# An earlier load of the third pair of heads, and a projection one step later in causal attention

## The reference

```python
x = LN(x + L0_attn(x))          # one wide attention with rotary embedding, K = 512
x = LN(x + L0_xattn(x, ctx, ctx, gamma))
#   q, k, v are [B, 512, 512]; 8 heads over the first axis (64 rows each):
#   qk = einsum('bhdq,bhdl->bhql', qh, kh) / sqrt(64); softmax; einsum('bhql,bhdl->bhdq', sm, vh)
x = LN(x + L0_ffn(x))           # ternary weights, 8-bit activations, Hadamard transform
x = LN(x + L1_attn(x))
#   kqv = x @ Wqkv + bqkv; 16 heads of 32
#   scores = einsum('bsnh,btnh->bnst', k, q) / sqrt(32)
#   scores = triu(scores) + -10000 * tril(ones, k=-1); softmax over axis 2; @ v; @ Wo + bo
x = LN(x + L1_xattn(x, ctx, mask))
x = LN(x + L1_ffn(x))           # 4-bit weights
```

## Time and profile before

| | |
|---|---|
| three runs, median | 1651.87 us (1650.08 to 1654.97) |
| the profiled execution, its own time | 1652.51 us |
| its span | 1650.7 us |
| mean granted TensorE clock | 0.981 |
| PE busy | 1546.3 us (94%) |
| DVE busy | 1276.7 us (77%) |
| ACT busy | 950.2 us (58%) |
| POOL busy | 761.9 us (46%) |

### The profile page before, as it was taken

The page is one execution under the profiler, slowest core; times in us unless marked ns, Lnnn a source line. Parts: engine busy times, 40 slices in busy tenths (PEclk is TensorE's granted clock), DMA queues, the critical chain, the costliest instruction groups (busy, mean ns, idle before and its releaser), DMA issues. The chain is left out here.

```text
span 1650.7 us, 25463 instructions
## 1 busy us (share of the span) xinstructions
PE 1546.3 (94%) x8236; PEld 1105.7 (67%) x8268; DVE 1276.7 (77%) x2288; ACT 950.2 (58%) x1980; POOL 761.9 (46%) x729
## 2 busy tenths in 40 slices
PE   8999998999987999999898999999899999999996
PEld 5788876666644566666666767676467767777774
DVE  6467665777989999997677687887779989767573
ACT  3212224787876677677566666666535555555654
POOL 5043255777832454452622233233144266656564
PEclk9999999999999999999997999999999999999998
DMA  7200016643220000003422122222243100000000
GB/s 229 77 1 26 1 51 172 211 129 117 65 77 1 1 1 1 2 1 77 117 77 59 57 77 58 59 77 65 66 119 96 47 1 1 1 26 26 1 26 26
DMA packets 66998, 95.95 MB, mean 58 GB/s; under 512 B 11956, under 2 KB 28852, under 8 KB 66868
## 3 DMA queue, kind: packets, MB, share of 16 engines
q1 hardware_dynamic: 60196, 81.47, 16.2%
q0 software_dynamic: 6144, 12.60, 2.9%
q10 hardware_dynamic: 528, 0.26, 0.1%
HBM read 56.53 MB, written 4.19 MB: 37 GB/s over the span
## 5 line engine op out<-in xcount | busy, mean ns | idle before, releaser
L1929 ACT ACTIVATE causal_probs<-bank,causal_neg 128x512 f32<-128x512 f32 (+3 forms) x256 | 134.4, 530 | 129.1 <-DVE causal_neg L2023 104.0
L3202 PE MATMUL bank<-fp_xT,fp_weights_values 128*128 128x512 f32 x704 | 187.7, 403 | 7.4 <-DVE fp_gate L3096 5.1
L3202 PEld LDWEIGHTS bank<-fp_xT,fp_weights_values 128*128 128x128 f32 x704 | 128.2, 188 | 55.0 <-DVE fp_gate L3096 12.3
L1196 POOL DMA_DIRECT2D causal_qS<-causal_qk x96 | 48.7, 514 | 190.3 <-DVE causal_qk L1188 143.0
L3229 PE MATMUL bank<-fp_wd,fp_hT 128*128 128x512 f32 x528 | 133.7, 393 | 1.4 <-POOL fp_hT L2919 1.1
L3105 DVE SCALAR_TENSOR_TENSOR fp_up<-bank,fp_weights_scales,fp_up 128x512 f32<-128x512 f32 x132 | 99.1, 751 | 44.8 <-ACT fp_up L2988 37.4
L892 DVE TENSOR_REDUCE heads_neg<-bank 128x1 f32<-128x512 f32 x128 | 86.3, 676 | 42.0 <-PE bank L943 41.8
L3229 PEld LDWEIGHTS bank<-fp_wd,fp_hT 128*128 128x128 f32 x528 | 98.5, 188 | 25.7 <-issue 3.4
L1627 PE MATMUL bank<-weights_raw,ternary_qT 128*128 128x512 bf16 x432 | 103.9, 386 | 6.2 <-DVE ternary_z L1468 5.4
L1255 POOL TENSOR_TENSOR ternary_z<-ternary_z 128x1024 f32<-128x1024 f32 x16 | 38.8, 2426 | 152.2 <-DVE ternary_z L1468 143.0
L355 POOL TENSOR_TENSOR rope_qk<-rope_rot 128x512 f32<-128x512 f32 x32 | 43.0, 1342 | 142.8 <-DVE rope_rot L458 141.3
(11 more groups left out here) (289 smaller groups left out, 4270.2 us busy)
## 6 DMA issues: line engine op xcount, KB each, us to landing
pairs_xd<-X SPq DMA_DIRECT2D x64, 128.0 KB, 2.6
pairs_cd<-in_ctx SPq DMA_DIRECT2D x64, 128.0 KB, 2.7
causal_qS<-causal_qk SPq DMA_DIRECT2D x96, 64.0 KB, 2.7
causal_qS<-causal_qk POOLq DMA_DIRECT2D x96, 64.0 KB, 2.5
causal_kS<-causal_qk SPq DMA_DIRECT2D x96, 64.0 KB, 2.7
causal_kS<-causal_qk POOLq DMA_DIRECT2D x96, 64.0 KB, 2.6
X<-in_x SPq DMA_DIRECT2D x4, 1024.0 KB, 6.8
heads_cT<-in_ctxT SPq DMA_DIRECT2D x4, 1024.0 KB, 5.7
```

Of the source, the lines that this page charges most:

```text
L1929: act.activation(probs_of(i)[:, h + one], view[:, one], ACT.Exp, bias=neg[:, G % 2, at:at + 1], accum_out=total[:, G % 2, at:at + 1]).then ...
L3202: last = pe.matmul(banks[4 + g][:], values[:, g, n % NI, of], xT[:, part, g], start=part == 0, stop=part == 1)
```

## The change

Two things. The third pair's load moves from the second stage's SP stream to the end of the first stage's; it waits for `stacked >= 1`, since it goes into pair 0's slot. And for G = 4, 8, 12 the queries' thirds are done in steps 1, 2, 3 in place of 0, 1, 2; ACT's high and DVE's low part of q follow in step 4 in place of 3. The keys stay in 3, 4, 4. `late` goes; the order of the streams is otherwise unchanged. Within ACT's step the high part stands behind the copies of turned tiles and ahead of the exponentials; within DVE's step the low part stands behind the maxima.

```diff
@@ rope_attention, SP
             pairs.load(sp, 0)
             pairs.load(sp, 1)
+            sp.wait_ge(pairs.stacked, 1)
+            pairs.load(sp, 2)
@@ head_attention, SP
             for g in range(PAIRS):
                 b, pair = divmod(g, NT)
-                if g >= 2:
+                if g >= 3:
                     sp.wait_ge(pairs.stacked, g - 1)
                     ...
                     pairs.load(sp, g)
@@ causal_attention
     PROJECT = ((0, 1, 2), (3, 4, 4))
+    PROJECT_NEXT = ((1, 2, 3), (3, 4, 4))
...
-        def late(G):
-            return 0
+        def thirds(G, j):
+            return (PROJECT if G % NF else PROJECT_NEXT)[j]
@@ ACT
-                if G + 1 < GROUPS and k - late(G + 1) in (PROJECT[0][-1] + 1, PROJECT[1][-1] + 1):
-                    first.high(act, G + 1, ...)
+                for j in range(2):
+                    if G + 1 < GROUPS and k == thirds(G + 1, j)[-1] + 1:
+                        first.high(act, G + 1, j, bank_of(G + 1, j))
@@ DVE
-                if G + 1 < GROUPS and k - late(G + 1) in (PROJECT[0][-1] + 1, PROJECT[1][-1] + 1):
-                    first.low(dve, G + 1, ...)
+                for j in range(2):
+                    if G + 1 < GROUPS and k == thirds(G + 1, j)[-1] + 1:
+                        first.low(dve, G + 1, j, bank_of(G + 1, j))
@@ PE
                 if G + 1 < GROUPS:
                     for j in range(2):
                         for third in range(3):
-                            if k == PROJECT[j][third] + late(G + 1):
+                            if k == thirds(G + 1, j)[third]:
                                 project(G + 1, j, third)
```

More of the change, by code:

```diff
@@ L1960, in _ @@
                         keep((n - TURN[u] - 1) // STEPS, u)
-                if G + 1 < GROUPS and k - late(G + 1) in (PROJECT[0][-1] + 1, PROJECT[1][-1] + 1):
-                    first.high(act, G + 1, (PROJECT[0][-1] + 1, PROJECT[1][-1] + 1).index(k - late(G + 1)), bank_of(G + 1, (PROJECT[0][-1] + 1, PROJECT[1][-1] + 1).index(k - late(G + 1))))
+                for j in range(2):
+                    if G + 1 < GROUPS and k == thirds(G + 1, j)[-1] + 1:
+                        first.high(act, G + 1, j, bank_of(G + 1, j))
                 for f in range(NF):
@@ L2090, in _ @@
                         keep(G, 0)
-                if G + 1 < GROUPS and k - late(G + 1) in (PROJECT[0][-1] + 1, PROJECT[1][-1] + 1):
-                    first.low(dve, G + 1, (PROJECT[0][-1] + 1, PROJECT[1][-1] + 1).index(k - late(G + 1)), bank_of(G + 1, (PROJECT[0][-1] + 1, PROJECT[1][-1] + 1).index(k - late(G + 1))))
+                for j in range(2):
+                    if G + 1 < GROUPS and k == thirds(G + 1, j)[-1] + 1:
+                        first.low(dve, G + 1, j, bank_of(G + 1, j))
                 for past_b, t, half in out_at(n):
```

## The result

Six runs of the changed kernel have a median of 1641.65 us (1640.24 to 1642.82), six of the kernel before beside them 1650.97 (1645.79 to 1654.97). The ratio is 0.9947, 95% interval 0.9932 to 0.9961: by the ratio 8.7 us faster, between 6.4 and 11.2 (the medians lie 9.3 apart). A second measurement in another session gave 0.9953 (0.9937 to 0.9970). Of the 4.8 us between the forecast and the median, 0.9 lie in the median before: the forecast started from 1651.87, of three runs, and six gave 1650.97.

The account below looks back on a forecast made before the run. PE was taken to bound both stages touched. The earlier load (-4.4) and later queries (-1.1) summed to -5.5 us: 1647.0 from the profiled 1652.51, expected median 1646.4, range 1642.8 to 1649.8 (forecast's own 1645 to 1648).

Parts of the forecast that it names:

- part 1: Head attention: the earlier third-pair load removes PE's 3.16 us wait at pair 2 and its slowness; -4.4 us in sum.
- the slow pair 2: Head attention: pair 2 takes 13.86 us, 1.23 more than in rhythm; this goes with the low clock.
- Rival C: Head attention: pair 3 takes the wait over, its loads behind 3 MB; gives back up to 3, 1649.5 us; chance 0.08.
- the forecast's own rule: Clock: about 3.7 us at low level cost 1.23, so a 6.7 us stretch costs 2.2 to 3.35 us.
- the end of the wait did not move: Causal attention, G = 4: x_low comes as before, so PE can't begin the first third before 872.30; 6.08 gain excluded.
- For G = 8 and 12 0.3 each: Causal attention: moved score and transposes gain 0.6 us per group; q's later low part leaves about 0.3 each.
- the copies at G = 4: First score of G = 4 waits for SP's k copies, which can move forward by 0.2 us or so.
- the step "That leaves 0.5 for G = 4": Causal attention, G = 4: the step keeps some 1.0 us, but k copies at the group's end leave 0.5.
- B: Rival: both parts at full and clock returns at G = 4, worth 1.2 to 1.7; -8.1, 1643.8 us; chance 0.20.
- low clock in other stretches, more than 3 us in sum: Sign that the forecast is wrong: low clock elsewhere than before, with more than 3 us in sum.

Follow-up runs that it names:

- experiment 4: Changed kernel with the queries' thirds in steps 1, 2, 2 or in steps 2, 2, 3 in place of 1, 2, 3: ratios 0.9965 and 0.9968 to the kernel before.
- after_fill: Changed kernel plus two useless matmuls in PE's wait ahead of the first projection of G = 4: ratio 0.9968 to the kernel before.
- experiment 3: Useless matmuls in the hole at G = 4: five in the kernel before 0.9989, two in the changed kernel 0.9968, five with the early load 0.9948.
- load_only: Kernel before with only the earlier load of the third pair: ratio 0.9970 to the kernel before, about -5.0 us.
- load_fill: Kernel before with the earlier load and five useless matmuls ahead of G = 4's first projection, old order of thirds: ratio 0.9948 to the kernel before.
- experiment 2: Each part alone, and both, against the kernel before: earlier load 0.9970, later queries 0.9978, both 0.9953.
- q_from2: Changed kernel with the queries' thirds in steps 2, 2, 3 in place of 1, 2, 3: ratio 0.9968 to the kernel before.
- before_fill: Kernel before plus five useless matmuls in PE's wait ahead of the first projection of G = 4: ratio 0.9989 to the kernel before.
- before_again: Kernel before, word for word, run once more for a second trace: ratio 1.0009, span 1650.7 us.
- later_only: Kernel before with only the queries' later thirds: ratio 0.9978 to the kernel before, about -3.6 us.
- before_fill_again: Kernel before with the five useless matmuls ahead of G = 4's first projection, once more: ratio 0.9973 to the kernel before.

## Why the prediction was right or wrong

**Right: part 1.** Every step held. The wait went wholly (3.2 us), so did the slow pair 2 (1.2 us), the eight issues ran from 248.3 to 253.2, POOL and PE came within 0.5 us of the times worked out, and pair 3 took no wait over. Alone it measured -5.0 us with an interval of 2.6 to 7.1. Rival C did not come. One reading beside the sum was off: the low clock in the window of the earlier trace rows is 3.4 us (0.57 of full over 4 us), not 3.7, so by the forecast's own rule a stretch of 6.7 us costs 2.4 at the least and not 2.2.

**Right: the end of the wait did not move.** PE's first third at G = 4 came 1.0 us behind the start of the group's first exponential before (871.34, 872.30) and after (864.70, 865.66). Only work moved into the hole counts, not the 6.1 us of waits. For G = 8 and 12 0.3 each was forecast and 0.42 and 0.38 measured: DVE and ACT hold what is left, as said, though q's later low part is only 0.06 of it.

**Right as an event, wrong as a price: the copies at G = 4.** The forecast said that the releaser of G = 4's first score would become a copy of k, and it did, with 1.67 us. I took that wait for lost time. In that trace it is not: the next score waits for ACT's exponentials whether the first is early or late (experiment 4), and DVE and ACT have no idle time from it. The term came true where the clock stayed at full: in after_fill the copies took back about 0.65 us (experiment 3). So 0.5 was a fair size for it, in the wrong case. I had looked at the first wait behind the edit and not at the second.

**Wrong: the step "That leaves 0.5 for G = 4".** Measured: group 3 2.35 us shorter in the first trace, and 2.2 to 2.35 between all traces that are alike ahead of it. (Groups 2 and 3 together are 2.0 to 2.8 shorter, 48.13 to 48.23 against 45.46 to 46.10; the 2.8 has the chance of group 2 in it.) The step left out the granted clock. I had put the clock's return in a rival (B, chance 0.20) as something that might help; it came in three traces of three with the new order and nothing else (and in the two of experiment 4), and in none of three with the old. The low stretch is 3.4 us shorter. At half speed that is at most 1.7 us; what remains, at least 0.5 to 0.65, is the score and the turn, forecast at 1.0 less 0.5 for the copies. How the two divide is not settled finer.

That the clock, and not the moved work as such, carries most of it is what the filling shows: it moves nothing, and group 3 loses 2.9 us by it between load_only and load_fill, with 6.8 us less of low clock. Moved work is not worthless at full clock, though. Groups 7 and 11, at full clock in every trace, gained 0.42 and 0.38 from it; at G = 4 the copies of k stand in the way.

**Chance, not change.** In the first pair of traces another 2.7 us come of low stretches that fell elsewhere: 1.4 in group 0, 0.8 in group 4, 0.5 before the causal stage. The forecast had named low clock in other stretches, more than 3 us in sum, as a sign of being wrong: 496 and 527 are such (3.4 us each), but what lies ahead of the causal stage sums to 13.6 us in both traces. A low stretch near 800 us is in two of the six traces of experiment 2, with and without the early load. In the medians such things are averaged: -5.0 and -3.6 for the parts, 7.6 in sum from the traces (4.4 + 2.35 + 0.80), and 7.8 to 8.7 measured. What the rest, up to a microsecond, is made of stays open; it is inside the intervals.

So of the 3.2 us by which the gain forecast (5.5) missed that of the first measurement (8.7), about 1.9 are the step at G = 4, 0.2 the other two groups, and about 1 is not told apart from noise.

The rule of the Trainium skill that was weighed (TensorE: Matmul & The Clock Gate, Part 1, What's actually happening: activity windows that run freely) agrees with what two executions of one kernel show: a low stretch at 541 us in one and at 803 in the other. The same section of the Trainium skill says that activity is what releases the throttle; here that shows as 10.2 us of low clock with nothing in the hole, 6.8 with useful work, and none, none and 3.4 with five matmuls of filling.

## What to carry to other kernels

Price a hole on TensorE with the clock that surrounds it: look at the granted clock on both sides of a wait, and count the low stretch that a shorter hole would give back. When the moved work ends at a later wait, follow one wait further before calling that time lost. When two traces are compared, look first whether their low stretches ahead of the place lie alike. A program can be faster by doing more on its busiest engine, where small waits let the clock fall.

## What the runs showed of the hardware

The same hole of 3 us on TensorE had 10.2 us at 1.2 GHz around it when nothing ran in it (three traces), 6.8 with scores and transposes in it (five traces: one score and four transposes in four, twice that in q_from2), and none, none and 3.4 with five matmuls that nobody needs. In the three unfilled traces of the old order the fall came ahead of the hole, behind waits of 0.92 and 0.58 us; but four of the filled traces have the same two waits there and no fall.

Small waits went with a fall where they stood close together. Around the start of group 2 (about 840 us) PE waits 0.94 us and, 1.8 us later, 0.5 to 0.7 us. In all 13 traces in which nothing filled these waits the clock fell 0.8 to 2.1 us behind the end of the first of them, for 3.4 or 6.8 us. At the start of group 4, with 0.94 and 0.35 to 0.71 us of wait, or with one of 1.65 to 2.77 us for the copies, it fell in 12 of the 13. It fell at neither place in the one trace in which three matmuls stood at each. From the start of group 5 to that of group 14 no wait is longer than 0.44 us but those at the first thirds (1.52 us each in the old order, 0.54 in the new), and in none of the 14 traces does the clock fall there.

At pair 2 waits of 2.92, 3.64 and 3.90 us were followed by a low stretch (before, before_fill, before_again), those of 2.50 and 2.61 (later_only, before_fill_again) were not.
